# Reordering the set-up of a conv and linear-attention kernel: statistics of image 0, selections, weights and the load of image 1

## What is computed

```
x = x + attention(group_norm(x))      # RMS norm over channels times g, w_qkv,
                                      # 4 heads of 32, softmax of q over d and of k over n,
                                      # 4 memory keys and values, w_out, b_out
x = x + conv(group_norm(x))           # 3x3 weights where (j - i) % 4 == 0,
                                      # 1x1 weights elsewhere, bias = sum of b over its rows
```

## Time and profile before

| | before |
|---|---|
| median of 3 runs | 2064.62 us |
| the profiled execution | 2065.06 us, its span 2063.2 us |
| busy share of the span | PE 93%, DVE 85%, ACT 66%, POOL 66% |
| image 0 in, weights in (start of the DVE instruction that waited) | 15.62 us, 26.39 us |
| scale and shift of image 0 done | 31.71 us |
| first broadcast of the inverse norm | 48.05 us |

### The profile page before, as it was taken

One profiled execution on the slowest core, in us unless ns is written; L12 is line 12 of the kernel. 1 busy time (PEld: TensorE's weight loads), 2 busy tenths in 40 slices (PEclk: granted clock), 3 DMA queues, 4 the chain that ended last, 5 costly groups with the idle time before them and its releaser, 6 DMA issues.

```text
span 2063.2 us, 50607 instructions
## 1 busy us (share of the span) xinstructions
PE 1913.9 (93%) x21199; PEld 1013.4 (49%) x21199; DVE 1750.3 (85%) x3144; ACT 1354.0 (66%) x1476; POOL 1362.4 (66%) x737
## 2 busy tenths in 40 slices
PE   2889999999999999999999999999999999999996
PEld 0445445555445555444555544555544555554552
DVE  5689888888988888988888988888988888898863
ACT  2567666767667767667676766676766776766761
POOL 5566666766667766667676667676666676666762
PEclk9789999999999999999999999999999999999997
DMA  5357777887767887667787777778777778876665
GB/s 105 62 127 147 154 149 158 168 169 153 149 154 160 169 168 158 151 148 160 169 158 165 154 152 153 162 164 173 149 151 151 159 168 171 154 151 147 144 136 127
DMA packets 349427, 312.96 MB, mean 152 GB/s; under 512 B 299152, under 2 KB 299920, under 8 KB 341008
## 3 DMA queue, kind: packets, MB, share of 16 engines
q1 hardware_dynamic: 347712, 308.73, 72.1%
q10 hardware_dynamic: 1168, 0.98, 0.2%
q0 software_dynamic: 320, 0.01, 0.0%
HBM read 68.10 MB, written 67.11 MB: 66 GB/s over the span
## 4 chain that ended last, share of the span: by engine, by line
PE 45%; DVE 36%; ACT 12%; POOL 3%; issue 1%; DMA 1%; ACTq 0%; SPq 0%
PE pair_ps L765 8%; DVE km L1114 7%; DVE u L1111 7%; PE pair_ps L802 7%; PE pair_ps L745 5%; DVE image L1166 4%; DVE nrm L1101 4%; DVE parts L1101 3%; PE bank_ps L699 3%; POOL exp_kT_lo L447 3%; PE bank_ps L775 3%; PE pair_ps L768 3%; PE pair_ps L793 3%; DVE part L1100 2%; PE bank_ps L754 2%; PE bank_ps L757 2%
## 5 line engine op out<-in xcount | busy, mean ns | idle before, releaser
L802 PE MATMUL pair_ps<-replicas,w_rep 96*32 96x512 f16 x8192 | 488.9, 383 | 7.9 <-DMA replicas<-yg_lo 7.9
L444 POOL TENSOR_TENSOR u_lo<-u,u_hi 128x1024 f16<-128x1024 f32 x128 | 269.9, 2144 | 270.3 <-ACT u_hi L551 270.3
L447 POOL TENSOR_TENSOR exp_kT_lo<-exp_kT,exp_kT_hi 128x1024 f16<-128x1024 f32 x128 | 300.2, 2354 | 178.9 <-ACT exp_kT_hi L560 178.8
L802 PEld LDWEIGHTS pair_ps<-replicas,w_rep 96*32 96x32 f16 x8192 | 205.8, 96 | 263.2 <-issue 77.8
L450 POOL TENSOR_TENSOR u_lo<-exp_q,u_hi 128x1024 f16<-128x1024 f32 x128 | 272.7, 2143 | 88.8 <-ACT u_hi L566 85.3
L1166 DVE SCALAR_TENSOR_TENSOR image<-pair_ps,image 128x512 f32<-128x512 f32 x256 | 172.5, 682 | 123.5 <-PE pair_ps L802 119.8
L440 POOL TENSOR_SCALAR u<-image,st 128x1024 f32<-128x1024 f32 x128 | 187.4, 1475 | 109.2 <-DVE st L1065 109.2
L551 ACT ACTIVATE u_hi<-u 128x1024 f16<-128x1024 f32 x128 | 130.8, 1045 | 173.3 <-DVE u L1111 173.1
L557 ACT ACTIVATE exp_kT<-pair_ps,zcol 128x1024 f32<-128x1024 f32 x128 | 141.0, 1102 | 144.0 <-PE pair_ps L745 144.0
L566 ACT ACTIVATE u_hi<-exp_q 128x1024 f16<-128x1024 f32 x128 | 135.3, 1057 | 137.1 <-DVE exp_q L1153 130.5
L536 ACT ACTIVATE exp_kT<-u,zcol 128x1024 f32<-128x1024 f32 x128 | 146.0, 1143 | 93.2 <-POOL u L440 92.2
(11 more groups left out here) (179 smaller groups left out, 4716.5 us busy)
## 6 DMA issues: line engine op xcount, KB each, us to landing
image<-in_x SPq DMA_DIRECT2D x256, 256.0 KB, 4.8
out<-image SPq DMA_DIRECT2D x512, 128.0 KB, 2.2
replicas<-yg_hi SPq DMA_DIRECT2D x256, 165.0 KB, 3.9
replicas<-yg_hi SPq DMA_DIRECT2D x256, 107.2 KB, 5.1
replicas<-yg_lo SPq DMA_DIRECT2D x128, 165.0 KB, 4.4
replicas<-yg_lo SPq DMA_DIRECT2D x128, 107.2 KB, 3.8
uT_hi<-u_hi SPq DMA_TRANSPOSE x128, 3.4
uT_lo<-u_lo SPq DMA_TRANSPOSE x128, 3.4
```

The lines of the kernel that those rows point to most:

```text
L444: pool.tensor_tensor(px(UL, v), px(U, v), px(UH, v), ALU.subtract).then_inc(ul_ready, 1)
L447: pool.tensor_tensor(KL[:, v % 2], KT[:, v % 2], KH[:, v % 2], ALU.subtract).then_inc(kl_ready, 1)
L802: mm = pe.matmul(conv_ps[32 * r:32 * r + 32, j % 2], w_rep[0:32 * SLOTS, tap, r], rep[:, j * ROWS + dy:(j + 1) * ROWS + dy, dx:dx + SIDE], ...
```

## The change

SP issues image 0, waits until both halves of it have arrived, and only then issues image 1. DVE no longer permutes weights: after `x_moments` it goes directly to `x_seed` and `x_scale`, and waits for the weights only then. ACT permutes the weights in three instructions ahead of step 0. POOL no longer writes the zeros of `spread` and `minus_max`; DVE does, ahead of `BIASES_READY`. PE turns the qkv and output weights first and signals, and then the ten conv matrices, now in `pair_ps[2]` and `pair_ps[1]`. ACT copies those from PSUM to a new scratch `taps32` in `B[2]` after `norm_power` of image 0, and rounds them after the last `high_u` of image 0. DVE makes the conv weights (`split_conv_weights`) after `rows_q` of image 0, in step 1, no longer in the set-up. SP sends them to `w_rep` after step 1, no longer after step 0. DVE builds `wqk_hi` and `wqk_lo` directly from PSUM. Besides, the order of two neighbouring waits is exchanged at nine places in the steps of SP, POOL, PE and DVE; one of them is shown.

```diff
+SPREAD_MADE = 16
+POOL_STEPS = 17
+BIASES_READY = 4
+PRODUCTS_READY = 9
+SETUP_READY = 14
+TAPS_TURNED = 2
+TAPS_KEPT = 5
+TAPS_ROUNDED = 6
...
+        taps32 = B[2][:, 13 * P:23 * P].rearrange("p (t c) -> p t c", t=TAPS + 1)
+        mid32 = B[2][:, 23 * P:25 * P].rearrange("p (t c) -> p t c", t=2)
...
-            for k in range(PRELOADED):
-                load(k, 0)
-                load(k, 1)
+            load(0, 0)
+            load(0, 1)
+            for h in range(2):
+                sp.wait_ge(x_in[h][0], at_load(0))
+            load(1, 0)
+            load(1, 1)
...
-            make(pool.memset(spread[:], 0.0))
+            pool.wait_ge(setup_dve, BIASES_READY)
             for part_no in range(3):
                 make(pool.affine_select(out=spread[:], in_=spread[:], compare_op=ALU.not_equal, fill=1.0,
...
+            act.activation(idle[:, 0:1], zcol[:, 0:1], ACT.Copy)
...
-            def norm_power():
+            def norm_power(s):
                 act.activation(nrm[:], nrm[:], ACT.Exp, scale=-0.5, bias=zcol[:, 1:2]).then_inc(norm_act, 1)
+                if first(s):
+                    act.wait_ge(setup_pe, TAPS_TURNED)
+                    act.activation(taps32[:, 0:8], conv_ps.rearrange("p k (t o) -> p (k t) o", o=P), ACT.Copy,
+                                   scale=W_SCALE).then_inc(setup_act, 1)
+                    act.activation(taps32[:, 8:10], pair_ps[1][:, 0:2 * P].rearrange("p (t o) -> p t o", o=P), ACT.Copy,
+                                   scale=W_SCALE).then_inc(setup_act, 1)
...
+                if first(s) and v == UNITS - 1:
+                    act.wait_ge(setup_act, TAPS_KEPT)
+                    act.activation(w_hi, taps32[:, 0:TAPS], ACT.Copy).then_inc(setup_act, 1)
...
+            act.wait_ge(weights_in, 16 * WEIGHT_DMAS)
+            act.activation(perm_qkv, raw_qkv.rearrange("p t (i r) -> p t r i", r=RES), ACT.Copy).then_inc(setup_act, 1)
+            act.activation(perm_w1, raw_w1.rearrange("p (i r) -> p r i", r=RES), ACT.Copy).then_inc(setup_act, 1)
+            act.activation(perm_w3, raw_w3.rearrange("p (i r t) -> p t r i", r=RES, t=TAPS), ACT.Copy).then_inc(setup_act, 1)
             over_samples(step)
...
             def turn_weights():
+                pe.wait_ge(setup_act, 1)
                 for t in range(3):
...
+                last.then_inc(setup_pe, 1)
+                pe.wait_ge(setup_act, 3)
                 for t in range(TAPS + 1):
...
                 if first(s) and v == 0:
-                    pe.wait_ge(setup_dve, SETUP_READY)
-                    pe.wait_ge(const_made, POOL_STEPS)
+                    pe.wait_ge(setup_dve, PRODUCTS_READY)
+                    pe.wait_ge(setup_act, TAPS_KEPT)
+                    pe.wait_ge(const_made, SPREAD_MADE)
...
                 if c is not None:
+                    pe.wait_ge(hi_in[0], at(c, 16 * 2 * RES, 16 * 2 * RES))
                     pe.wait_ge(lo_in[0], at(c, 16 * RES, 16 * RES))
-                    pe.wait_ge(hi_in[0], at(c, 16 * 2 * RES, 16 * 2 * RES))
                     conv_ring(c, 0)
...
+            def split_conv_weights():
+                dve.wait_ge(setup_act, TAPS_ROUNDED)
+                make(dve.tensor_tensor(mid32[:, 0], taps32[:, CENTRE], quad_mask[:], ALU.mult))
+                make(dve.tensor_tensor(mid32[:, 1], taps32[:, TAPS], other_mask[:], ALU.mult), wait=True)
+                make(dve.tensor_tensor(mid32[:, 1], mid32[:, 1], mid32[:, 0], ALU.add), wait=True)
+                make(dve.tensor_copy(w_mid[:, 0], mid32[:, 1]), wait=True)
+                dve.tensor_tensor(w_mid[:, 1], mid32[:, 1], w_mid[:, 0], ALU.subtract)
+                make(dve.tensor_tensor(w_lo, taps32[:, 0:TAPS], w_hi, ALU.subtract))
...
                 dve.tensor_copy(qmT[:], ps[:, 0:P // 2].bitcast(BF16)).then_inc(q_max, 1)
+                if first(s):
+                    split_conv_weights()
...
+            dve.memset(minus_max[:], 0.0)
+            make(dve.memset(spread[:], 0.0))
             assert made == BIASES_READY
...
-            dve.wait_ge(weights_in, 16 * WEIGHT_DMAS)
-            make(dve.tensor_copy(perm_qkv, raw_qkv.rearrange("p t (i r) -> p t r i", r=RES)))
-            make(dve.tensor_copy(perm_w1, raw_w1.rearrange("p (i r) -> p r i", r=RES)))
-            for t in range(TAPS):
-                last = dve.tensor_copy(perm_w3[:, t], raw_w3.rearrange("p (i r t) -> p t r i", r=RES, t=TAPS)[:, t])
-            make(last)
             dve.wait_ge(x_group, 1)
             x_seed(0, bank_ps[1])
             dve.wait_ge(x_stat, 8)
             x_scale(0)
+            dve.wait_ge(weights_in, 16 * WEIGHT_DMAS)
...
```

More of the change, by code:

```diff
@@ L66 @@
 SMALL_CONSTANTS = 13
-POOL_STEPS = 19
-BIASES_READY = 3
-WEIGHTS_READY = 6
-SETUP_READY = 15
+SPREAD_MADE = 16
[6 more added lines that the diff above has]
+TAPS_ROUNDED = 6
 WEIGHT_DMAS = 1 + 4 * RES
@@ L166, in build @@
         mvT = sb("mvT", [P, P])
-        wqkvT = sb("wqkvT", [P, 3, P])
+        wvT = sb("wvT", [P, P])
         wqk_h = sb("wqk_hi", [P, 2, P], F16)
@@ L281, in image, with over_samples @@
             return B[buffer_of(sample)]
-        def over_samples(step, after_first=None):
+        def over_samples(step, after_second=None):
             def known(s):
@@ L289, in over_samples @@
                 step(known(s), known(s - 1), known(s - 2), known(s - 3))
-                if s == 0 and after_first is not None:
-                    after_first()
+                if s == 1 and after_second is not None:
+                    after_second()
         block = ctx.enter_context(nc.Block())
@@ L352, in step @@
                     if e is not None:
+                        sp.wait_ge(stored[0], at(e, 16 * RES, 16 * RES))
+                    if e is not None:
                         sp.wait_ge(stored[1], at(e, 16 * RES, 16 * RES))
-                    if e is not None:
-                        sp.wait_ge(stored[0], at(e, 16 * RES, 16 * RES))
                     load(p, 0)
@@ L372, in step @@
                     if e is not None:
+                        sp.wait_ge(stored[2], at(e, 16 * RES, 16 * RES))
+                    if e is not None:
                         sp.wait_ge(stored[3], at(e, 16 * RES, 16 * RES))
-                    if e is not None:
-                        sp.wait_ge(stored[2], at(e, 16 * RES, 16 * RES))
                     load(p, 1)
@@ L664, in step @@
                     act.wait_ge(norm_act, at(p, 2, 1))
-                    norm_power()
+                    norm_power(p)
                     act.wait_ge(u_ready, at(p, UNITS, 1))
@@ L670, in step @@
                     square_y(a, 0)
-            act.wait_ge(setup_pe, 1)
-            for t in range(0, TAPS, 4):
-                n = min(4, TAPS - t)
-                last = act.activation(w_hi[:, t:t + n], tap_ps(t, n).rearrange("p (t o) -> p t o", t=n), ACT.Copy,
-                                      scale=W_SCALE)
-            last.then_inc(setup_act, 1)
+            act.wait_ge(weights_in, 16 * WEIGHT_DMAS)
+            act.activation(perm_qkv, raw_qkv.rearrange("p t (i r) -> p t r i", r=RES), ACT.Copy).then_inc(setup_act, 1)
+            act.activation(perm_w1, raw_w1.rearrange("p (i r) -> p r i", r=RES), ACT.Copy).then_inc(setup_act, 1)
+            act.activation(perm_w3, raw_w3.rearrange("p (i r t) -> p t r i", r=RES, t=TAPS), ACT.Copy).then_inc(setup_act, 1)
             over_samples(step)
@@ L761, in queries @@
             def queries(s, v, ps):
+                if first(s) and v == 0:
+                    pe.wait_ge(const_made, POOL_STEPS)
                 for j in (2 * v, 2 * v + 1):
@@ L820, in value_context @@
             def value_context(ps):
-                pe.matmul(ps[:, 0:P], wqkvT[:, 2], AT_sb[:], start=True, stop=False)
+                pe.matmul(ps[:, 0:P], wvT[:], AT_sb[:], start=True, stop=False)
                 pe.matmul(ps[:, 0:P], mvT[0:MEM], pkT_sb[0:MEM], start=False, stop=True).then_inc(mix_pe, 1)
@@ L1092, in y_scale @@
                 scale_shift(1, chain(y_stat, s, Y_STEPS, 9))
+            def split_conv_weights():
[6 more added lines that the diff above has]
+                make(dve.tensor_tensor(w_lo, taps32[:, 0:TAPS], w_hi, ALU.subtract))
+                assert made == SETUP_READY, made
             def norm_guard(s, ps):
```

65 lines of the change are left out of this document (24 added, 41 removed).

## The result

The changed kernel takes 2053.20 us (median of four runs, 2052.82 to 2054.18) against 2065.39 us of the kernel before (2064.17 to 2067.15): ratio 0.9941, 95% interval 0.9924 to 0.9958. So it is faster by more than 0.2%, as forecast, and 1.8 us under the 2055.0 that I named. Its profiled execution took 2054.18 us, and its span is 10.8 us shorter than in the earlier trace rows.

The account below looks back on a forecast made before the run. PE's own work plus a little of DVE's bounds the image loop; savings in the serial set-up move the whole program. Set-up -11.1 plus split 1.5 gives -9.6 us off the median 2064.62: 2055.0 us, range 2050.5 to 2060.5.

Parts of the forecast that it names:

- The path through the set-up: Set-up chain from image 0 to the norm's guard: guard at about 30.9 instead of 42.02, 11.1 us earlier, bounds 9 and 12.
- Part 3: Weights in set-up: in at 18.0 (bounds 17, 20), ACT permutes in 2.0 us, conv matrices permuted at 20.0 (19 to 24).
- The first rival: Set-up: ACT permutes in 8 us or weights land late; norm sums move 3.4 us, gain 6.2, 2058.4 us; chance 0.14.
- Part 1: Image 0's statistics in set-up: without weights ahead, x_seed and x_scale end at about 22.3 instead of 31.71, 9.4 us earlier.
- Part 5: DVE's conv weight split in step 1, ahead of image 1's statistics: path lengthens 0 to 1.9 us, taken as 1.5.
- The clock: PE's granted clock, half level after idling: return to full speed may shift against the work; taken as 0, 2.5 us in range.
- The exchanged waits: Nine swapped wait pairs in the steps: PE waits at none in the middle; cost 0, bounds -1.5 and +3 us.
- the rival: Every image: swapped waits change DVE and POOL's order at L1161 (yg_lo), PE waits longer; slower, 2069 us; chance 0.04.
- the two last terms: Split in step 1, cost 1.5 us, and granted clock in early steps, cost 0 with 2.5 us in the range.
- SP's queue: Twelve w_rep DMAs, 7.95 us, now between step 1 and image 2's load: cost nothing, with 26 us of cover.

Follow-up runs that it names:

- Experiment two: Kernel before, with only x_seed and x_scale of image 0 moved ahead of DVE's wait for the weights: 2068.09 us, ratio 1.0011.
- load and zeros: Kernel before, with only image 1 held back until image 0 is in and the two memsets given to DVE: 2058.31 us, ratio 0.9967.
- experiment one: Kernel before, with only image 1 held back until image 0 is in: 2063.36 us, ratio 0.9989.
- six: Changed kernel, with the weights permuted by DVE's eleven copies behind x_scale instead of by ACT: 2058.19 us, ratio 0.9969.
- after_load_early: Changed kernel, with image 1 loaded at once again, as before: 2060.81 us, ratio 0.9979.
- Experiment seven: Changed kernel, with the largest instruction of the conv weight split (1152 columns) run three times instead of once: 2060.60 us, ratio 0.9980.
- taps_late: Changed kernel, with 3x3 weight DMAs issued after image 0, ahead of image 1, and conv transposes behind the norm sums: 2051.86 us, ratio 0.9934.
- experiment nine: Changed kernel, with 61 unneeded matmuls added in PE's idle times: 2046.59 us, ratio 0.9911.
- POOL's zeros: Changed kernel, with both memsets given back to POOL: 2056.52 us, ratio 0.9958.
- Experiment eight: Changed kernel, with all nine exchanged pairs of waits put back in the old order: 2053.10 us, ratio 0.9947.

## Why the prediction was right, and where its steps were not

| place | predicted | measured |
|---|---|---|
| weights in | 18.0 | 18.99 |
| first `x_seed` | 19.6 | 20.03 |
| POOL's constants end | 20.8 | 20.85 |
| first POOL unit | 22.5 | 23.00 |
| transposes end | 23.1 | 24.79 |
| first norm sum | 24.9 | 25.43 |
| guard | 30.9 | 30.89 |
| first broadcast | 37 | 36.91 |
| cost of the split | 1.5 | 0 |
| clock | 0 (bounds ±2.5) | 0.9 by the third image |
| median | 2055.0 | 2053.20 |

**The path through the set-up** is right in its order and within about half a microsecond at each step of the chain; the weights and the transposes, which are not on it, were 1.0 and 1.7 late. The half microsecond is image 0: its second half was in at 16.10 instead of 15.62. I had said that it could hardly lose. In the set-ups of the other kernels with the same DMAs it was in between 15.4 and 16.2, and between 15.61 and 16.16 in three whose set-up is the same up to there, so this is scatter. That the guard came out exact is luck: the norm sums started 0.5 us late and took 5.46 us to it (25.43 to 30.89) instead of my 6.0, and in the other kernels with this permutation that way took 4.7 to 6.0.

**Part 3, the permutation on ACT, was mis-sized.** I priced 1664 columns by contiguous data at 2.0 us. The three took 18.99 to 22.33, 3.3 us. The row of 1152 strided columns took 2.23 us where the same engine takes 1.15 for 1152 contiguous ones (L564, above, which writes float16 and not float32): twice as long. With the weights 1.0 later than I took them, the transposes ended 1.7 later than forecast, and of the 1.8 us to spare 0.64 were left. The first rival had this cover fail at 8 us of permutation; it would have begun to fail at 4.0, 0.64 more than was measured, though its full price of 3.4 us was far.

**Part 1 had the right sum and the wrong owner.** I wrote 9.4 us beside the statistics, and made the other parts conditions that cost nothing. Experiment two shows that the edit alone loses 2.5 us at the guard. The guard of the kernels between (42.02 before; 39.26 with the load; 35.19 with load and zeros; 36.35 with all but ACT's permutation; 30.89 with all) gives 2.8, 4.1 and, for the last two together, 4.3. With the load and the zeros in place, all the rest of the change without ACT's permutation makes it 1.16 us worse; no run adds the statistics alone at this point. The parts depend on each other because DVE's copies of 128 columns and its two-operand subtractions take turns with POOL: 1.70 us for nine copies alone, 6.70, 3.41 and 4.26 beside POOL (experiments one, two, six). The Trainium skill (SBUF — State Buffer, "Who interferes with whom") says that a DVE copy in a two-port mode and GpSimd exclude each other for whole instructions, whoever comes first. The four durations agree with it, and so does the single copy of 4.68 us in experiment one; in which mode these copies run, the profile does not say, and the copy of 384 columns did not wait (0.84 us beside the selection). ACT, which the page calls free of such waits, shows none: its 1152 columns took 2.23 us, of which 0.75 lay beside POOL's selection, and 2.24 at 27.53 in `after_load_early`, where POOL had ended at 27.36. I had read that rule for the subtraction in step 1 only, though it decides the set-up: the eleven copies of before ran in the one place where POOL was idle, from 25.4 to 31.9.

**Part 5, the split, was 1.5 us too dear.** Five small instructions and their waits took 1.3 us, close to my estimate of 1.5. The large one took 1.35 instead of up to 3.08, because it started at 63.39, 0.19 us ahead of POOL's subtraction; the turn was POOL's to wait (5.26 us for two, where they take 4.26). I had it start at 75.0 in the times of before, 0.1 behind POOL's 74.90. A distance of 0.3 us between two instructions decided 1.8 us, and the rows that I had did not fix it that closely. It is no chance of one run: in every kernel with this split the first of these instructions took 1.35 us. Experiment seven shows the price of the other order: 3.17 us each. My sentence that the group means would come behind DVE's moments was wrong for the same reason: the moments were done 0.53 us before PE had finished its queries. The cover was 0.5 us as the durations say, and behind it every microsecond counts in full.

**The clock: 0.9 us of the shift were lost by the third image.** The shift is 11.13 at the guard, 11.28 at the second `krow` and 10.23 at the third. Between these, the last half stretch runs from 100.6 to 117.7, in the times of before 111.7 to 128.8, while the stretch in before was 109.6 to 126.7: it lies 2.1 us later against the work. The other profiles bear this out. The way from the second key row to the third takes 64.25 to 64.49 us in the four kernels whose last half stretch ends 7.0 to 7.5 us behind the second key row (the changed kernel, `after_perm_dve`, `after_old_waits`, `taps_late`). It takes 63.40 to 63.44 in the seven where that stretch ends 4.4 to 5.2 us behind it, the kernel before among them. In experiment nine, where the stretch has ended before this key row, it takes 61.38. No run moves the stretch alone, so this is a match over thirteen profiles and not a separate test. From guard to third `krow` the other kernels without more matmuls lose between 0 and 1.0 us against the kernel before (0.24 with the load alone, 0.28 with load and zeros, 0.0 with POOL's zeros, 0.9 with late taps, 1.0 with the old waits), leaving out the long split, and none gains. So my bounds of 2.5 us were too wide by a factor of more than two.

**The exchanged waits: the rival's mechanism took place, and its price in the middle was zero.** I feared that they would change who starts first at L1161. They did, the other way round: DVE's median fell from 2150 to 1289 ns, POOL's mean rose from 2495 to 2943. DVE was relieved of 51 us over the run and spent them mostly waiting for PE's group means (8.6 to 29.7 us in the window of the middle), since PE's waits in the middle hardly changed at the four places. The step of the rival that failed is its link from this row to PE: up to the last image the row is not on PE's path, in neither direction, by 0.9 us in the median instruction. Experiment eight turns it back in the same time. Only in the last image does the new order reach PE, and there it helps by about 1 us in the profiles.

**The sum.** The errors of the two last terms have opposite signs: 1.5 too dear, 0.9 too cheap. From the key row of image 2 on, the shift of 10.2 is 0.6 more than forecast; the span is 10.8 shorter, and the medians differ by 12.2, of which 0.8 is the kernel before, now at 2065.39 with one more run. Of the span's 10.8, 9.7 are there at the 32nd key row; the last 1.1 come behind it, with the new order of the waits (experiment eight). I had cost 0 for that. Left open is one slip of 0.6 us near the 16th image in the profile of the changed kernel (PE's single 0.3 us wait at L827 lies there). From the third key row to the 32nd the thirteen profiles take 1779.5 to 1781.1 us, with either order of the waits, and 1780.3 in the changed kernel: the period from image to image did not change, and slips up to this size occur in both orders.

**SP's queue** behaved as forecast: the 12 DMAs are issued at 64.8 to 72.7, image 2 behind them, and no engine waits for them.

## What to carry to other kernels

Before moving an instruction of VectorE that copies, or that has two operands in SBUF, look in GpSimd's timeline at what lies beside its new place: a chain of nine copies took two to four times as long there, and that made a good edit a loss until a second edit moved the neighbour. Try the parts of a joint change alone and in pairs before crediting one of them, since here the part that seemed to carry the gain was slower by itself. And when the head of a program is serial and TensorE idles in it, look at the granted clock behind the gaps: a few dozen unneeded matmuls in them were worth as much here as half of the whole change.

## What the hardware showed that I had not expected

- Nine DVE copies of 128 columns: 1.70 us undisturbed, 3.41 to 6.70 beside POOL's selection or group norm. One copy that began 0.1 us behind a selection of 4.67 us took 4.68 instead of 0.26. A memset of POOL held such copies too (0.95 and 0.84 us). A copy of 384 columns was held by neither, with 0.82 to 0.85 us in every kernel that has it on DVE.
- ACT copies 1152 strided columns in 2.23 us and 1152 contiguous ones, to float16, in 1.15.
- DVE writes the zeros of `minus_max` in 1.76 us and of `spread` in 0.48, where POOL takes 3.51 and 0.95; the profile shows DVE's as half as many 32-bit words.
- An exchange of neighbouring waits turned round which of DVE and POOL goes first at `yg_lo`: DVE's median went from 2150 to 1289 ns, POOL's mean from 2495 to 2943.
- 61 matmuls in PE's gaps cut the time at the half level of the granted clock (1.2 of 2.4 GHz) between 35.8 and 117.7 us from 47.8 to 17.0 us, and the run by 6.6 us.
- Four DMAs of weights on another queue hold up image 0 by about a microsecond: without these four beside it its second half is in at 14.48 and 14.52, with them between 15.4 and 16.2.
